# Routed experts of a mixture-of-experts layer: 128×128 weight blocks held in the array and all 128 gathered tokens streamed, in place of token blocks held and weights streamed

## The reference

```
def _swiglu_ffn(x, wg, wu, wd):
    return jax.nn.silu(x @ wg) * (x @ wu) @ wd
...
for e in range(E):                      # E = 64, wg, wu: 512 x 512, wd: 512 x 512
    routed = routed + _swiglu_ffn(x, Wg[e], Wu[e], Wd[e]) * gate[:, e:e + 1]
out = (shared + routed + x)
```

## Time and profile before

| what | before |
|---|---|
| median of 3 runs | 995.87 us (992.62 to 999.44) |
| profiled execution | 995.54 us |
| its span | 993.6 us |
| TensorE busy | 855.6 us (86%) |
| VectorE, ScalarE, GpSimd busy | 547.5, 255.4, 286.5 us |
| mean granted TensorE clock | 0.947 |
| HBM traffic | 319 GB/s over the span |

### The profile page before, as it was taken

How to read it: one execution, slowest core, us unless ns; L and a number is a source line. 1 busy time by engine, 2 the same in 40 slices (tenths; PEclk the granted TensorE clock), 3 DMA queues, 4 the chain that set the end, 5 groups by cost and what they waited for, 6 DMA issues and landing times. The chain is left out here.

```text
span 993.6 us, 21562 instructions
## 1 busy us (share of the span) xinstructions
PE 855.6 (86%) x7785; PEld 551.1 (55%) x7785; DVE 547.5 (55%) x1625; ACT 255.4 (26%) x573; POOL 286.5 (29%) x271
## 2 busy tenths in 40 slices
PE   2488887977685789999999989999999999999990
PEld 1243454534342776666565666667666666656660
DVE  7998999999889873333232423333324333333216
ACT  2112111211401222232222222332233222223230
POOL 5675443433001012222222222223222222222111
PEclk9689999988888799999999999999999999999996
DMA  8765687656489706989889999999987999999976
GB/s 277 259 190 192 214 267 228 204 187 194 153 229 396 290 17 242 343 345 387 330 290 359 369 402 408 378 356 404 383 321 294 401 401 380 377 371 375 400 269 229
DMA packets 76935, 300.76 MB, mean 303 GB/s; under 512 B 13730, under 2 KB 14119, under 8 KB 58548
## 3 DMA queue, kind: packets, MB, share of 16 engines
q1 hardware_dynamic: 57256, 254.21, 67.6%
q0 software_dynamic: 17280, 38.48, 12.1%
q10 hardware_dynamic: 2252, 6.06, 1.7%
HBM read 290.26 MB, written 26.62 MB: 319 GB/s over the span
## 5 line engine op out<-in xcount | busy, mean ns | idle before, releaser
L1236 DVE TENSOR_TENSOR arena<-arena 128x288 f32 (+1 forms) x640 | 235.1, 441 | 14.0 <-POOL spare L715 4.4
L1871 PE MATMUL bank<-arena,low 128*64 128x256 f32 x2048 | 240.7, 383 | 1.4 <-issue 1.4
L1871 PEld LDWEIGHTS bank<-arena,low 128*64 128x64 f32 x2048 | 139.9, 137 | 75.1 <-issue 12.8
L1712 PE MATMUL bank<-arena,multi 128*32 128x256 f32 x1584 | 119.7, 436 | 59.9 <-DVE arena L1236 59.8
L1896 PE MATMUL bank<-arena,low 128*64 128x256 f32 x1392 | 161.3, 379 | 1.1 <-ACT low L993 1.1
L756 POOL DMA_INDIRECT low<-xr_d,idx x64 | 90.4, 1412 | 240.7 <-DVE place L1467 178.2
L760 POOL DMA_INDIRECT y_d<-low,place x64 | 68.0, 1062 | 262.1 <-ACT low L1000 181.4
L1896 PEld LDWEIGHTS bank<-arena,low 128*64 128x64 f32 x1392 | 101.4, 137 | 50.2 <-ACT low L993 1.3
L1712 PEld LDWEIGHTS bank<-arena,multi 128*32 128x32 f32 x1584 | 60.1, 124 | 114.5 <-issue 48.4
L693 POOL DMA_INDIRECT arena<-xn_d,ssel x79 | 107.9, 1366 | 36.7 <-issue 21.8
L1000 ACT ACTIVATE low<-bank,gcol 64x256 f32<-64x256 f32 x174 | 81.8, 470 | 105.7 <-PE bank L1896 104.6
(11 more groups left out here) (220 smaller groups left out, 718.3 us busy)
## 6 DMA issues: line engine op xcount, KB each, us to landing
arena<-in_L_ffn_Wg_dram SPq DMA_DIRECT2D x64, 1024.0 KB, 9.2
arena<-in_L_ffn_Wu_dram SPq DMA_DIRECT2D x64, 1024.0 KB, 11.5
arena<-in_L_ffn_Wd_dram SPq DMA_DIRECT2D x64, 1024.0 KB, 8.9
arena<-in_edge_attr_dram SPq DMA_DIRECT2D x88, 256.0 KB, 4.6
arena<-y_d SPq DMA_DIRECT2D x5, 1250.0 KB, 6.4
sums_d<-arena ACTq DMA_DIRECT2D x18, 256.0 KB
arena<-sums_d SPq DMA_DIRECT2D x4, 896.0 KB
arena<-in_L_mix_W_qkv_dram SPq DMA_DIRECT2D x2, 1024.0 KB, 18.8
```

Of the source, the lines that this page charges most:

```text
L1236: return dve.tensor_tensor(prod[:, buf, 0:n, EXT * p:EXT * p + EXT], x1[b][:, 0:n, bass.ds(i1, EXT)], x2[b][:, 0:n, bass.ds(i2, EXT)], ALU ...
L1712: ins = pe.matmul(bank[2 * b + c // 2][at:at + 32, 256 * (c % 2):256 * (c % 2) + 256], pair[:, pairs, i, 32 * s:32 * s + 32], prod[:, buf, ...
L1871: ins = pe.matmul(out_bank[64 * h:64 * h + 64, w * HF:(w + 1) * HF], xgT[:, b, k, 64 * o:64 * o + 64], gu[:, slot, w, k, h * HF:(h + 1) * HF],
```

## The change

For every expert all 128 gathered rows are computed, with no branch on the count. `gate_or_up` holds a 128×128 block of the weights and streams the 128 token columns of `xgT`, so its output is h already turned, four blocks of 128 hidden columns beside each other in one bank; 16 matmuls for gate and 16 for up. The two h transposes, the copy of hT, the second half's path (`gate_and_up_part`, `part_transpose`, the second `down`) and the flags in registers are gone. `down` holds 128 columns of hT and streams 512 weight columns, 4 matmuls. SiLU, multiply and scale each work on 128×512 in one instruction. Gate has a semaphore and a bank of its own. SP's reloads wait for `s_G` and `s_U`, and the down weights come in stretches of 2 KB (row `c p`).

```
-CAP = 64
-CAP2 = 2 * CAP
-PART = 32
-HF = D // 2
+CAP = 128
...
     def load_down(slot, w):
-        sp.dma_start(dn[:, slot].rearrange("p (h c) n -> p h c n", h=2),
-                     w.rearrange("(h p c) n -> p h c n", h=2, c=2)).then_inc(s_wd[slot], 16)
+        sp.dma_start(dn[:, slot], w.rearrange("(c p) n -> p c n", c=DC)).then_inc(s_wd[slot], 16)
...
                 if i < NX:
-                    sp.wait_ge(s_xgTp, e + 3)
+                    sp.wait_ge(s_G, e + 1)
                     load_gate(i % GU_RING, wg[i])
+                    sp.wait_ge(s_U, e + 1)
                     load_up(i % GU_RING, wu[i])
...
+            def silu(b):
+                return act.activation(sg, bank[GATE_BANK[b]][:, :], ACT.Silu)
+
+            def scale(i, b):
+                return act.activation(yy[:, b, :], bank[5][:, :], ACT.Copy, scale=gcol[:, i:i + 1])
...
+            def mult(b):
+                return dve.tensor_tensor(hT[:, b].rearrange("p c n -> p (c n)"), sg, bank[UP_BANK[b]][:, :], ALU.mult)
...
-            def gate_or_up(o, b, slot, w, out_bank):
+            def gate_or_up(b, slot, w, out_bank):
+                for c in range(DC):
+                    for k in range(DC):
+                        ins = pe.matmul(out_bank[:, c * CAP:(c + 1) * CAP], gu[:, slot, w, k, c * 128:(c + 1) * 128], xgT[:, b, k, :],
+                                        start=(k == 0), stop=(k == DC - 1))
+                return ins
...
+            def down(b, slot):
                 for k in range(DC):
...
+                    ins = pe.matmul(bank[5][:, :], hT[:, b, k, :], dn[:, slot, k, :], start=(k == 0), stop=(k == DC - 1))
                 return ins
...
-                if e >= 1:
-                    ov = pe.snap(over[(e - 1) % 16], min_val=0, max_val=NX)
-                    pe.wait_ge(s_h, e)
-                    h_transpose(0, bank[2]).then_inc(s_hTp, 1)
                 if e < NX:
                     pe.wait_ge(s_xgT, e + 1)
...
                     pe.wait_ge(s_wg[slot], 16 * fill)
-                    gate_or_up(0, e % 2, slot, 0, bank[GU_BANK[e % 2]])
...
+                    gate_or_up(e % 2, slot, 0, bank[GATE_BANK[e % 2]]).then_inc(s_G, 1)
...
                     pe.wait_ge(s_wu[slot], 16 * fill)
...
+                    gate_or_up(e % 2, slot, 1, bank[UP_BANK[e % 2]]).then_inc(s_U, 1)
                 if e >= 1:
                     pe.wait_ge(s_wd[last], 16 * last_fill)
...
+                    pe.wait_ge(s_h, e)
...
                     if e >= 2:
                         pe.wait_ge(s_ys, e - 1)
-                    down(0, last, bank[5]).then_inc(s_y, 1)
...
+                    down((e - 1) % 2, last).then_inc(s_y, 1)
```

More of the change, by code:

```diff
@@ L1022, in _ @@
                         act.wait_ge(s_scat[(e - 1) % 2], 16 * ((e - 1) // 2))
-                    with act.If(0 < ov):
-                        hold(act, "act", o_y, ov & UPTO)
-                        scale(1, bank[OV], (e - 1) % PLACES, (e - 1) % 2).then_inc(o_ys, 1)
                     act.wait_ge(s_y, e)
[L1027 to L1036, removed]
+                    scale((e - 1) % PLACES, (e - 1) % 2).then_inc(s_ys, 1)
                 if AFTER.get(e, ("", 0))[0] == "up":
                     shared_silu(AFTER[e][1])
-            n_extra = act.value_load(vrow[:, NX:NX + 1], min_val=0, max_val=MAX_EXTRA)
+            act.wait_ge(s_flags, 1)
+            n_extra = act.value_load(extra_v[:, :], min_val=0, max_val=MAX_EXTRA)
             with act.If(0 < n_extra):
@@ L1461, in index @@
                 dve.tensor_tensor(idx[:, i:i + 1], look[:, 1:2], t1, ALU.add).then_inc(s_idx, 1)
-                for o in range(2):
-                    for h in range(2):
-                        dve.tensor_reduce(gcol[64 * h:64 * h + 64, i, o:o + 1], look[64 * o:64 * o + 64, 4:7], AX, ALU.add)
+                dve.tensor_reduce(gcol[:, i:i + 1], look[:, 4:7], AX, ALU.add)
                 dve.wait_ge(s_idx, i_seen[0] + 1)
@@ L1521, in _ @@
                 dve.wait_ge(s_sg, e + 1)
[L1522 to L1530, removed]
+                dve.wait_ge(s_U, e + 1)
+                if e >= 2:
+                    dve.wait_ge(s_y, e - 1)
+                mult(e % 2).then_inc(s_h, 1)
                 if e in AFTER:
@@ L1563, in _ @@
                         look = bank[0][:, 384:384 + LOOK]
[L1564 to L1566 removed]
+                        dve.tensor_reduce(gcol[:, 0:1], look[:, 4:7], AX, ALU.add)
                         dve.tensor_scalar(idx_t[:, 0, 0:1], look[:, 2:3], -float(FAR), float(FAR), ALU.mult, ALU.add).then_inc(s_idx01, 1)
@@ L1866, in h_transpose @@
                 return ins
-            def gate_or_up(o, b, slot, w, out_bank):
+            def down(b, slot):
                 for k in range(DC):
-                    for h in range(2):
-                        ins = pe.matmul(out_bank[64 * h:64 * h + 64, w * HF:(w + 1) * HF], xgT[:, b, k, 64 * o:64 * o + 64],
-                                        gu[:, slot, w, k, h * HF:(h + 1) * HF],
-                                        start=(w == 0 and k == 0), stop=(k == DC - 1), skip_group_check=True)
-                return ins
@@ L1876, in gate_and_up_part @@
-            def gate_and_up_part(q, b, slot, out_bank):
-                for k in range(DC):
-                    for w in range(2):
-                        for h in range(2):
-                            at = 64 * w + PART * h
-                            ins = pe.matmul(out_bank[at:at + PART, q * HF:(q + 1) * HF], xgT[:, b, k, CAP + PART * q:CAP + PART * (q + 1)],
-                                            gu[:, slot, w, k, h * HF:(h + 1) * HF], start=(k == 0), stop=(k == DC - 1), skip_group_check=True)
-                return ins
@@ L1920, in _ @@
                 lookup(e % 2, rtab[:, e]).then_inc(s_look, 1)
-            GU_BANK, OV = (3, 4), 6
-            over = [pe.alloc_register(f"pe_over{i}") for i in range(2 * PLACES)]
-            over2 = [pe.alloc_register(f"pe_over2_{i}") for i in range(2 * PLACES)]
             pe.wait_ge(s_xg[0], 16)
@@ L1964, in _ @@
+                    if e == 1:
+                        pe.wait_ge(s_flags, 1)
+                    pe.wait_ge(s_wu[slot], 16 * fill)
+                    gate_or_up(e % 2, slot, 1, bank[UP_BANK[e % 2]]).then_inc(s_U, 1)
                 if e >= 1:
                     pe.wait_ge(s_wd[last], 16 * last_fill)
-                    with pe.If(0 < ov):
-                        hold(pe, "pe", o_hT, ov & UPTO)
-                        down(1, last, bank[OV]).then_inc(o_y, 1)
-                    pe.wait_ge(s_hT, e)
+                    pe.wait_ge(s_h, e)
```

159 lines of the change are left out of this document (35 added, 124 removed).

## The result

| | before | after |
|---|---|---|
| median of 4 runs each | 994.25 us (990.40 to 999.44) | 1187.85 us (1186.52 to 1188.74) |
| profiled execution, its span | 995.54, 993.6 us | 1187.89, 1186.1 us |

The change makes the kernel slower by a ratio of 1.194, 95% interval 1.188 to 1.200. I had forecast 1239 us within 1212 to 1300, slower by 24%.

The account below looks back on a forecast made before the run. TensorE's own work was taken to bound the loop: +353 us for longer passes, −107.5 for large experts and −1.5 at the end, added to 995.5 us, gave 1239 us, slower by 24%, range 1212 to 1300 us.

Parts of the forecast that it names:

- What bounds the kernel: Routed loop: lasts as long as TensorE's own work; other engines and DMA fit under it, changes count one for one.
- the rivals: Weight load partly exposed (0.08); weight transfers late (0.03); one instruction per matmul, 892 us (0.02); loop really DMA-bound (0.04).
- the bound from below on gate and up: Gate and up: 128 streamed columns can't be quicker than runs with 64, 0.115 and 0.122 us an instruction.
- the term for gate and up: New gate and up in each pass: 64 instructions at 0.118 us, 7.55 us.
- Down: New down in each pass: 8 instructions streaming 512 columns at 0.442 us each, 3.54 us.
- joints: Between groups in a pass: 0.10 us added where a group waits for a semaphore and can't load weights ahead.
- transposes: Token transposes in each pass, four of 128 columns: 0.49 us.
- shared units: 26 in the loop: 16 of 2.93 us and 10 of 8 × 0.442 us.
- The loop before: Routed loop of the kernel before: 64 × 5.68 + 107.5 + 122 = 593 us.
- The large experts: Extra gate and up, transposes and second down for experts with over 64 rows: 107.5 us together, which goes.
- Costs at nothing: Multiply about 1077 ns, SiLU and scale about 586 ns, reloads and 16384 more DMA packets: all hidden beside other work.
- The end: After the loop: TensorE's 1.13 us idle for turned h goes, two scales become one: −1.5 us.

Follow-up runs that it names:

- cols64: Changed kernel, but from the third expert on gate and up stream only the first 64 of 128 token columns: 1186.65 us.
- held96cols64: Changed kernel, but from the third expert on gate and up hold 96 weight columns of each block and stream 64 token columns: 1080.98 us.
- held96: Changed kernel, but from the third expert on gate and up hold 96 of 128 weight columns and stream all 128 token columns: 1175.15 us.
- spare_tile: Changed kernel with two spare matmuls a pass from the third on, holding 64 columns in one half of the array: 1242.55 us.
- spare_full: Changed kernel with two spare full-width matmuls a pass from the third on, 128 columns held, 64 streamed: 1213.41 us.
- down_by_32: Kernel before, with the second down of large experts in blocks of 32 tokens, four side by side with 128 weight columns each: 1093.92 us.

## Why the prediction was wrong, point by point

- **What bounds the kernel:** right. TensorE's own work sets both, and what was added there came out one for one. None of the rivals came about; the granted clock stayed at 1.00 in the loop.
- **The step that failed: the prices taken from runs of records, and first of all the bound from below on gate and up**, "More columns can't be quicker", with 0.115 and 0.122 us from two rows. The logic is right (64 columns: 0.112 us, 128: 0.113), but the rows weren't the bare instruction, which is the 0.112 that its load takes. The run at 0.115 holds one change of tiling, and the 40 at 0.122, which hold 125 columns and not 128, ran at a mean granted clock of 0.90 (window 333.5 to 338.2; 0.55 in its first microsecond, 1.00 from 334.5 on), as I could have seen. So the term for gate and up was too large: 7.55 us forecast, 7.23 measured, 20.5 us over 64 passes.
- **Down, joints, transposes, shared units:** the same failing. The 0.442, the 0.10 "for waits at semaphores", the 0.49 and the 2.93 all held a change of tiling that the changed kernel, which never tiles in its loop, doesn't have. I ascribed it to semaphores. 19.3 us. By the forms of its records TensorE changes its tiling 198 times in the loop before, some three times a pass, and never in the loop after; at 0.117 us that is an estimated 23 us of the 602.
- **The loop before:** my 593 us was the sum of its instructions and missed 9.8 us of "issue" stops, which lie between them. A sum of the work should have been laid against the loop's own length, 602 us, in the trace; this would have shown 9 us to explain. The DMA share was read from two windows too: it is 0.97 there and 0.92 over the loop, so the demand was nearer 554 us than 575.
- **The large experts:** 107.5 us by rows. No run measured it alone, since with them gone the weights are late.
- **Costs at nothing:** right. The multiply took 687 ns, not 1077, the scale 687, not 586, all under cover. The row that I took for the multiply reads with a stride and the new one doesn't; that this is the reason wasn't tried. The packets were cheaper than either bound.
- **The end:** the 1.13 us of idle time stayed as 0.93, for another reason: down of the last expert waits for the scale of the one before to free its bank. The end still got 4.1 us shorter. Of VectorE's five sums over the scattered rows four are done by 1172.5 us and one is left (at 1174.87), where before three were done by 976.0 and two were left (at 977.03 and 982.62); that the slower passes give the earlier scatters this time is my reading.
- **The range:** its lower end had room for gate and up at 0.113 us, the value measured, which alone gives 1218 us. It had none for down, joints, transposes and shared units being too long as well (19.3 us), nor for the 9 us of the loop before; these together took the time out of it. All the errors pointed the same way, and the spread was worked out as if only gate and up could be off.

## What to carry to other kernels

When a price is taken from a run of instructions, subtract the first record by its own length, look at the minimum and maximum of the line, and at what stands before the run: a change of tiling cost 0.117 us here, as much as an instruction. Full width for experts that mostly have at most 64 rows costs 19 to 20% here, whichever operand is held; with 128×128 float32 blocks held, the load sets 0.112 us, with 64 columns streamed as with 128. And lay the sum of the work against the measured length of its stretch before the difference to the new kernel is made.

## What the runs showed of the hardware that I had not expected

- In these runs an instruction of a full-width float32 matmul takes the longer of its load and its stream: 0.112 us for 128 held (`cols64`) and 0.0855 for 96 (`held96cols64`), against 0.110 for 128 streamed (`held96`), and 0.177 for 209 and 0.429 for 512 (L1773 and L1809 of the changed kernel). Load and stream overlap in full width: L1773 streams 209 columns every 0.177 us with a load for each, where one after the other the two would take an estimated 0.112 + 0.174 us (209 × 0.83 ns).
- A change between full width and a 64-column tiling cost 0.114 to 0.117 us (`spare_tile` against `spare_full`), with the reserve said there.
- Four tiles of 32 side by side took 0.034 us an instruction at 128 columns, and 0.056 at 256 (3.59 us from start to start of 64, both in `down_by_32`).
- TensorE stopped for up to 4.0 us at a time on "issue" where code with branches ran beside a busy DMA: 9.8 us in the loop before (DMA share 0.92), 68.5 with one branch more a pass (0.83), none with branches in TensorE's program at a share of 0.70, none without branches at 1.00.
- Going from 4 KB to 2 KB stretches cost 0.9 ns of SP's queue time for each packet more, net, on a less loaded queue.
